# An early-fusion transformer block: y's low part on GpSimd, the projection's add split in two on VectorE, the first batch's statistics behind its decays, and w1's halves behind head 0's scaling

## What is computed

```
h = concat(tokens(x), txt)
q, k, v = LN(h) @ Wq.T, LN(h) @ Wk.T, LN(h) @ Wv.T
scores = (q @ k.T) / 8 * decay          # decay = gamma ** (m - l) above the diagonal, else 0
o = softmax(scores) @ v
o = (o - mean) / sqrt(var + eps)        # over all tokens and the 64 columns of a head
h = h + (o * gn_weight + gn_bias) @ Wo.T
h = h + sum over the 8 chosen experts of gate * (gelu(LN(h) @ w1) @ w2)
```

## Time and profile before

| what | value |
|---|---|
| median of 3 runs | 806.47 us (804.6 to 806.86) |
| the profiled execution's own time | 805.87 us |
| its span in the trace | 804.1 us |
| TensorE busy | 754.5 us (94%) |
| VectorE busy | 557.3 us (69%) |
| ScalarE busy | 480.1 us (60%) |
| GpSimd busy | 144.3 us (18%) |

### The profile page before, as it was taken

The page is one execution under the profiler, slowest core; times in us unless marked ns, Lnnn a source line. Parts: engine busy times, 40 slices in busy tenths (PEclk is TensorE's granted clock), DMA queues, the critical chain, the costliest instruction groups (busy, mean ns, idle before and its releaser), DMA issues.

```text
span 804.1 us, 13357 instructions
## 1 busy us (share of the span) xinstructions
PE 754.5 (94%) x4480; PEld 643.9 (80%) x4480; DVE 557.3 (69%) x1559; ACT 480.1 (60%) x1079; POOL 144.3 (18%) x249
## 2 busy tenths in 40 slices
PE   6669989989998889999999999999999999999997
PEld 2568878878887767888888888888888888888885
DVE  5678788888888776665666666566676666765654
ACT  1257877877888755556556456456455465554443
POOL 2043326326324483010010010010010100100000
PEclk9689999999999899999999999999999999999999
DMA  7500010010031253224223242241242342322410
GB/s 219 172 21 21 1 42 22 22 42 22 22 100 41 74 168 110 66 84 116 53 79 108 63 113 72 75 125 38 88 122 62 75 111 63 95 73 63 117 50 19
DMA packets 44391, 60.89 MB, mean 76 GB/s; under 512 B 4018, under 2 KB 37762, under 8 KB 44322
## 3 DMA queue, kind: packets, MB, share of 16 engines
q1 hardware_dynamic: 44322, 60.04, 26.4%
HBM read 51.97 MB, written 8.05 MB: 75 GB/s over the span
## 4 chain that ended last, share of the span: by engine, by line
PE 65%; issue 17%; POOLq 6%; POOL 5%; DVE 3%; ACT 2%; DMA 1%; DVEq 1%; SPq 0%
PE ps L1259 62%; POOL xn L472 2%; POOLq L526 1%; POOLq L498 1%; POOL w_lo L500 1%; ACT pr L668 1%; PE ps L1442 1%; POOL rstd L454 1%; DMA gate<-comb_dram 1%; POOLq L512 1%; POOLq L558 1%; POOLq L456 1%; PE ps L1391 1%; POOL y L527 1%; DVE act_lo L934 1%
## 5 line engine op out<-in xcount | busy, mean ns | idle before, releaser
L1165 DVE TENSOR_TENSOR act<-act,gate 128x480 f32<-128x480 f32 (+1 forms) x216 | 145.7, 675 | 115.9 <-ACT act L778 112.3
L1259 PE MATMUL ps<-x,w_hi 128*128 128x480 f32 (+1 forms) x648 | 217.0, 389 | 0.2 <-ACT act L778 0.2
L778 ACT ACTIVATE act<-ps 128x480 f32<-128x480 f32 (+1 forms) x216 | 123.7, 573 | 131.5 <-PE ps L1259 131.4
L1259 PE MATMUL ps<-x,w_lo 128*128 128x480 f32 (+1 forms) x432 | 165.9, 384 | 0.0
L934 DVE TENSOR_TENSOR act_lo<-act,act_hi 128x480 fp32r<-128x480 f32 (+1 forms) x216 | 145.7, 674 | 0.2
L1259 PEld LDWEIGHTS ps<-x,w_hi 128*128 128x128 f32 x648 | 121.6, 188 | 21.2 <-ACT act L778 0.7
L586 ACT ACTIVATE act_hi<-act 128x480 fp32r<-128x480 f32 (+1 forms) x216 | 130.8, 606 | 6.7 <-DVE act L1165 6.7
L1259 PEld LDWEIGHTS ps<-x,w_lo 128*128 128x128 f32 x432 | 81.2, 188 | 13.4
L1259 PE MATMUL ps<-act_hi,w_hi 128*128 128x480 f32 (+1 forms) x216 | 83.5, 387 | 5.6 <-DVE act_lo L934 5.6
L668 ACT ACTIVATE pr<-sc,nm 128x580 f32<-128x580 f32 (+4 forms) x120 | 66.4, 557 | 30.8 <-DVE nm L982 30.7
L1259 PE MATMUL ps<-act_hi,w_lo 128*128 128x480 f32 (+1 forms) x216 | 82.5, 382 | 0.0
(11 more groups left out here) (178 smaller groups left out, 1266.4 us busy)
## 6 DMA issues: line engine op xcount, KB each, us to landing
gate<-comb_dram SPq DMA_DIRECT2D x112, 240.0 KB, 3.2
gate<-comb_dram SPq DMA_DIRECT2D x32, 256.0 KB, 3.7
w_raw<-w SPq DMA_DIRECT2D x16, 384.0 KB, 3.6
h_dram<-h SPq DMA_DIRECT2D x8, 384.0 KB
res<-h_dram SPq DMA_DIRECT2D x7, 360.0 KB, 4.4
out<-res SPq DMA_DIRECT2D x7, 360.0 KB, 3.2
h<-txt SPq DMA_DIRECT2D x3, 672.0 KB
decay_rows<-drow SPq DMA_DIRECT2D x1, 1014.0 KB, 7.3
```

The costliest lines, as they stand in the source:

```text
L778: a.activation(act[j % 3][:, 0:n], ps[:, up_bank(j), 0:n], ACT.Gelu_apprx_tanh).then_inc(gelu_done, 1)
L1165: dve.tensor_tensor(act[j % 3][:, 0:n], act[j % 3][:, 0:n], gate[e % 4][:, 0:n], ALU.mult).then_inc(gated, 1)
L1259: return pe.matmul(dst, w, x, start=start, stop=stop)
```

## The change

Five edits, all in the attention part:

1. `y_values` on GpSimd also computes the lo parts of y (two subtractions, `y_lo`), for batches 0 to 5. VectorE's `y_rest` goes from `body`. It stays in the expert stage for batches 6 and 7. GpSimd now scales both halves of o first, then rounds both, then subtracts both.
2. `add_attention` takes the tiles to add: tile pair 0 where all three stood, pair 1 and the last tile behind the scaling of head 1.
3. In batch 0 both `norm_stats` move: that of batch 1 behind the decays of heads 0 and 1, that of batch 2 behind the scaling of head 1.
4. `halve_w1(b)` also waits for `probs_ready`, the end of head 0's scaling in batch b, and stands behind `rstd_of(b+2)` instead of ahead of it.
5. `gn_variance(t)` waits until y of batch t-1 is rounded.

```
             def halve_w1(b):
                 pool.wait_ge(ld_w1, nth(b, 16, 16))
+                pool.wait_ge(probs_ready, nth(b, H, 1))
...
+                o = ot[t % 2]
+                for i in range(2):
+                    pool.tensor_scalar(o[:, i, :], o[:, i, :], gscale[:, i:i + 1], gshift[:, i:i + 1], ALU.mult, ALU.add)
+                pool.drain()
                 for i, dst in enumerate((y01_hi, y2)):
-                    pool.tensor_scalar(ot[t % 2][:, i, :], ot[t % 2][:, i, :], gscale[:, i:i + 1], gshift[:, i:i + 1], ALU.mult, ALU.add)
-                    pool.drain()
-                    pool.tensor_copy(dst[:, :], ot[t % 2][:, i, :]).then_inc(y_hi, 1)
+                    pool.tensor_copy(dst[:, :], o[:, i, :]).then_inc(y_hi, 1)
+                pool.drain()
+                for i, (p0, lo, hi) in enumerate(((0, y01_lo, y01_hi), (HD, y2, y2))):
+                    if i:
+                        pool.drain()
+                    pool.tensor_tensor(lo[p0:P, :], o[p0:P, i, :], hi[p0:P, :], ALU.subtract).then_inc(y_lo, 1)
+                pool.drain()
...
-                halve_w1(b)
                 if ahead:
                     pool.drain()
                     rstd_of(b + 2, ln1_var, rstd, mv, veps, nmr, ln1_rstd)
+                halve_w1(b)
...
             def gn_variance(t, bank=GN_BANK):
                 dve.wait_ge(gn_sum, nth(t, 1, 1))
+                if t:
+                    dve.wait_ge(y_hi, nth(t - 1, 2, 2))
...
-                else:
-                    norm_stats(1, st6, mv, veps, ln1_var)
-                if ahead:
+                if tail and ahead:
...
-                if later:
-                    y_rest(b - 2)
...
                 apply_decay(b, 1)
+                if not tail:
+                    norm_stats(1, st6, mv, veps, ln1_var)
                 normalise(b, 0)
                 apply_decay(b, 2)
                 if later and more:
-                    add_attention(b - 2, WO_BANKS)
+                    add_attention(b - 2, WO_BANKS, (0,))
...
                 normalise(b, 1)
+                if later and more:
+                    add_attention(b - 2, WO_BANKS, (1, 2))
+                if not tail:
+                    dve.wait_ge(ln1_rstd, 2)
+                    norm_stats(2, st6, mv, veps, ln1_var)
```

## The result

The changed kernel takes 797.65 us (median of 4 runs, 796.21 to 798.31) against 806.38 us for the one before (4 runs): a ratio of 0.9893, 95% interval 0.9873 to 0.9914. The prediction was 796.2 us with a range of 791.5 to 801.0. The profiled execution took 798.31 us, its span is 796.5 against 804.1, so the traces have 7.6 us to account for.

What follows compares the result with a forecast made beforehand. A middle batch was taken as a loop through VectorE, whose order sets the pace, and TensorE. Terms 6.4 + 0.3 - 0.2 + 3.5 + 0.3 = 10.3 us off 805.87 gave 795.6, with 0.6 for the median 796.2 us (791.5 to 801).

Steps and rivals of the forecast that it cites:

- Edits 1 and 2, batches 2 to 5: Middle batches: y's low parts off VectorE and two adds moved gain 1.6 us a batch, 6.4 us (3.2 to 9.6).
- The price of the overlaps: Middle batches: GpSimd's work over VectorE's at four places costs 0.25 us each, 1.0 us a batch.
- first rival: Overlaps eat most of the gain: batches 2 to 5 gain about 0.8 each, total 800.7 us; chance 20%.
- The slower case: GpSimd's subtractions block VectorE's subtractions and statistics; six batches lose 2.7 us each, total 818 us; chance 4%.
- The weighed rule: Shared SBUF port as exclusive lock: each middle-batch overlap could last some 0.5 us, total near 799.8 us.
- Batch 6: Already at 28.01 us with 0.6 of TensorE's gap, so it gains 0.3 us (0 to 0.6).
- Batch 7: GpSimd's two subtractions come 0.4 late, the moved halving gives part back: 0.2 us lost (0.7 lost to 0.4 gained).
- Batch 1: The later halving mostly leaves head 2's scaling: 0.3 us gained (0.5 lost to 1.2 gained).
- Edit 3, batch 0: First batch: moving both statistics starts the decays 4.1 us earlier and gains 3.5 us (2.5 to 4.1).
- scores of three tiles are there at about 39.9: First batch: the decays start at 39.9 when these scores are ready, 4.1 us earlier.
- then TensorE's transposes of head 1: First batch: 1.8 us directly after head 1's scaling ends at 53.8, leading to column sums at 56.3.
- Tells: Signs to check in the trace, such as column sums near 56.3 and batches 2 to 5 at 28.1 to 28.7 us.

Runs made afterwards that it cites:

- e5_ylo_back: Changed kernel with y's low parts back on VectorE ahead of the decays: 802.50 us, 4.85 above the changed kernel.
- e4_halve_early: Changed kernel with w1's halving not waiting for head 0's scaling and again ahead of the rstd: 799.24 us, 1.6 above the changed kernel.
- e7_fill_halve_gn: Changed kernel with batch 1's statistics back behind k's low part, and w1's halving in batches 1 to 5 waiting for the group-norm partial sums: 794.31 us.
- e1_stats_back: Changed kernel with both first-batch statistics back ahead of the decays: 798.18 us, 0.5 above the changed kernel.
- e2_fill: Changed kernel with only batch 1's statistics back, directly behind k's low part: 794.28 us, 3.4 below the changed kernel.
- e3_halve_later: Changed kernel with w1's halving in batches 0 to 6 waiting for head 1's scaling instead of head 0's: 797.73 us.

## Why the prediction was right, and which step of it failed

The total came out inside the range, 1.45 us above the number by the medians. By the profiled executions, against which the sum was made, 7.6 us came off where 10.3 were forecast: batches 2 to 5 gave 1.4 more, batch 0 with its later start 2.9 less (2.1 less by its own length), and batches 1, 6, 7 and the expert stage together 1.2 less. That the total hit is in part luck: the middle batches gave more than forecast and covered a part of what batch 0 did not give. Counted by `xa_lo`, batches 2 to 5 gave 0.8 more and batch 1 0.3 more than forecast.

**Edits 1 and 2, batches 2 to 5: right, 7.8 by column sums or 7.2 by `xa_lo` instead of 6.4 us.** Both waits of TensorE went, as forecast, and two experiments tie the time to the edits: undoing y's part costs 4.85 us, the adds 2.6. Undoing the halving's move costs 1.6, but little of that here (0.45 for four batches by `xa_lo`). The price of the overlaps was right as a sum and wrong in each place. I took four times 0.25 = 1.0 us. The trace shows `veps` at 0.17, and `nm` at 0.39, 0.20 and 1.00, so 0 + 0.22 + 0.03 + 0.83 = 1.08. The mis-sized term is the last: I had 1.9 us for head 1's transposes and took 1.6 because ScalarE "gained only 1.6". The batches gained 7.78 / 4 = 1.94 by column sums and 7.18 / 4 = 1.80 by `xa_lo`. (In the first rival's sum, 3.3 us for batches 0 and 6 should read 3.8 by the forecast's own terms, which makes it 800.2 us.) The first rival, batches that gain 0.8, is out by these lengths. The slower case, in which the subtractions block VectorE, is out by the rows: they lie over `k_lo` and `st`, which kept their 1.55 and 1.38.

**The weighed rule.** What was held, in one run or another, is `nm` 128x4, `veps` (0.44 in `e5_ylo_back`), batch 1's scaling and batch 0's in `e4_halve_early`, which have one operand in SBUF and scalars, and `den` and `gmv`, which have two in SBUF. In the batches read, the decays, `k_lo` and `st` were not. That division is the one that the Trainium skill draws in "SBUF — State Buffer", section "Who interferes with whom", and the traces agree with it. My 799.8 us by that rule came from pricing each place at 0.5; the places hold between 0 and 0.83.

**Batch 6: right** (0.16 for 0.3). **Batch 7: small and on the right side** (0.35 for 0.2 lost); the further 0.55 in the expert stage stand beside a `gate` load that VectorE waited 0.5 longer for, and both are within the scatter of that part. **Batch 1: 0.08 lost for 0.3 gained by column sums, but 0.63 gained by `xa_lo`.** The second count is the one to trust, as the column sums behind it came early before. That `e7_fill_halve_gn` takes 26.87 us for this batch is the same effect, not more to win.

**Edit 3, batch 0: the step that failed, 3.5 us forecast.** The batch itself gained 1.36, and `e1_stats_back` shows the edit as a whole worth 0.5 us by the medians, which can't be told from nothing, and 1.0 by the traces. I had the column sums at 56.3; they start at 59.13. Of the 2.8 us between, the batch's later start is 0.72. Then "scores of three tiles are there at about 39.9": the decays started at 41.26, 0.64 later than that beyond the start. Of these, 0.36 is TensorE's slower clock ahead of the end of k's low part (10.29 us behind the second column sum, before 9.93) and no doing of the edit; VectorE then waited 2.31 us for the scores where I had 2.03. From there VectorE ran nearly as added up (53.8 to the end of head 1's scaling, against 55.34, is 1.54 in all). The remaining 1.4 is the step "then TensorE's transposes of head 1": they started at 56.72, not at 55.34, because TensorE was still at `pt,v`, at 1.2 GHz. I counted VectorE's time and left out what the statistics do to TensorE: a wait of 2.78 us where "near 1 us" was forecast, and the fall of the clock behind it. A row of my own showed the effect: the first matmul behind the 5.05 us wait took 0.79 us, the same matmul in a middle batch 0.50.

The larger error is one of choice. Ahead of the edit VectorE had, as I read it, 4.1 us of statistics and waits to lose, and I took it that both sets had to leave. The changed kernel's 2.31 us of idle time before the decays is room for one set of 2.05 us, and `e2_fill` uses it: 794.28 us, a ratio to the kernel before of 0.9855 [0.9841, 0.9868]. That is the best version found; `e7_fill_halve_gn` equals it.

**Tells.** Column sums of batch 1 near 56.3: no, 59.13. Batches 2 to 5 within 28.1 to 28.7: three of four (28.20, 28.20, 27.78, 28.65), and all four by `xa_lo`. Batch 6 at 27.7 to 28.0: yes. Waits of 1.34 and 0.46 gone: yes. Stretched `nm`: yes. Wait near 1 us in batch 0: it moved, 1.17 there and 2.78 at the next place.

## What to carry to other kernels

Before moving work off a wait, look at what the engine will then wait for: here 2.31 us of new idle time held one of the two moved pieces for nothing, and leaving that piece there was worth 3.4 us. Work set between two stages of one engine can be paid twice by the engine behind it, as a wait and as a lower clock after it. Where one engine is 97% busy (27.37 of 28.20), a stall of 0.8 us on another can be free, so take it away in an experiment before working on it. A mark that can come early and then wait, as the column sums here, moves time between two batches that neither has gained; check such a length with a second mark. And one trace of a batch at the start holds chance: the clock alone moved batch 0 by up to 2.0 us between kernels that are the same there.

## What the runs showed of the hardware

- VectorE's smallest instructions pay the most for their size when GpSimd runs: `nm` of four elements took 1.00 us instead of 0.17, `den` of five 0.83, `gmv` of two 0.88 instead of 0.16. Each ends where GpSimd's subtraction ends: `den` in `e4_halve_early` runs to 103.71 + 0.83 = 104.54, the subtractions from 102.53 for 1.99 to 104.52; `gmv` in `e3_halve_later` to 114.54, they to 114.53. So in these rows the price of an overlap is what is left of GpSimd's instruction, up to its whole 0.98 us, whatever the size of VectorE's. A group of several can lose more: head 1's scaling, five instructions, took 3.41 instead of 1.58 us under the halving's rounding and two subtractions (`e4_halve_early`). The `nm` of one element per partition took 154 ns on average over its 24 instances in the changed kernel, with GpSimd's scaling of the next input (127.95 for 2.42) over the one at 128.49, which took 0.15.
- TensorE went from 2.4 to 1.2 GHz behind a wait of 2.78 us that was followed by a short burst (0.60 us) and 0.83 us more; behind waits of 1.17, 0.75 and 0.82 us in `e2_fill` it stayed at 2.4. The eighteen `pt,v` matmuls took 2.73 us where the clock fell and 1.79 where it did not. The rise in batch 0 is not at a fixed place: the granted clock was 1.00 from 30 us on in `e4_halve_early` and 0.50 up to 34 us in the changed kernel, in front of any line in which they differ.
- GpSimd gains from the move as well: the copy of 128x320 behind the normalised input took 1.02 us in batch 3 of the kernel before, with VectorE's subtractions of y at 130.60 to 132.21 over it, and 0.45 in the changed kernel.
